# One layer-norm, Fourier-mixing and MLP block on one core: the MLP's products moved into one stretch of TensorE's program

## The reference

```python
x = box_conv_block(x)                       # layer 0
for l in range(4):                          # layer 1: four blocks
    residual = x                            # x is (4, 64, 128, 128)
    xn = layer_norm(x over channels)
    xf = rfft2(xn)
    o1 = relu(xf mixed by w1[l] over channels, complex)
    o2 = o1 mixed by w2[l] over channels, complex
    mask = (abs(o2.real) > 0.01) | (abs(o2.imag) > 0.01)
    x = residual + irfft2(o2 * mask)
    m = gelu(layer_norm(x) @ mlp_w1[l] + mlp_b1[l]) @ mlp_w2[l] + mlp_b2[l]   # 64 -> 256 -> 64
    x = x + m
x = box_conv_block(x); x = box_conv_block(x)   # layers 2 and 3
```

## Time and profile before

| | |
|---|---|
| device time, median of 3 runs (lowest to highest) | 3583.87 us (3582.81 to 3584.54) |
| the profiled execution, first to last instruction | 3583.9 us |
| TensorE busy | 3266.5 us (91%) |
| VectorE busy | 2413.5 us (67%) |
| ScalarE busy | 2339.5 us (65%) |
| GpSimd busy | 1656.8 us (46%) |
| mean granted TensorE clock | 0.964 of full speed |

### The profile page before, as it was taken

How to read it: one execution, slowest core, us unless ns; L and a number is a source line. 1 busy time by engine, 2 the same in 40 slices (tenths; PEclk the granted TensorE clock), 3 DMA queues, 4 the chain that set the end, 5 groups by cost and what they waited for, 6 DMA issues and landing times. The chain is left out here.

```text
span 3583.9 us, 53035 instructions
## 1 busy us (share of the span) xinstructions
PE 3266.5 (91%) x18285; PEld 1967.2 (55%) x18285; DVE 2413.5 (67%) x4148; ACT 2339.5 (65%) x3749; POOL 1656.8 (46%) x1389
## 2 busy tenths in 40 slices
PE   6946699999999999998999999999999999979689
PEld 2735464646474646464646464646464646334257
DVE  4956676767676667666767677677767674536677
ACT  3955576767676767677767676766666666646468
POOL 4445545454646454545454545555454543210242
PEclk7968899999999999999999999999999999989889
DMA  9850001010101010313120101111111111356898
GB/s 327 271 183 24 30 30 64 32 65 30 65 30 65 30 65 30 118 48 141 48 89 30 65 30 65 36 65 41 54 42 53 42 53 42 141 188 189 263 300 239
DMA packets 250281, 334.10 MB, mean 93 GB/s; under 512 B 22304, under 2 KB 195616, under 8 KB 242608
## 3 DMA queue, kind: packets, MB, share of 16 engines
q1 hardware_dynamic: 241664, 315.29, 26.0%
q0 software_dynamic: 7904, 15.57, 1.6%
q10 hardware_dynamic: 464, 0.02, 0.0%
HBM read 188.06 MB, written 142.74 MB: 92 GB/s over the span
## 5 line engine op out<-in xcount | busy, mean ns | idle before, releaser
L1546 ACT ACTIVATE images<-a_wide,a_up_b 128x1024 f32<-128x1024 f32 x512 | 569.0, 1111 | 137.0 <-PE a_wide L1728 135.6
L1728 PE MATMUL a_wide<-images 64*128 64x512 f32 x2048 | 579.9, 641 | 37.0 <-ACT images L1546 36.3
L1308 POOL TENSOR_TENSOR images<-a_o,a_mag 128x256 f32<-128x256 f32 (+1 forms) x512 | 365.1, 738 | 389.3 <-DVE a_mag L1410 389.3
L1739 PE MATMUL a_result<-images 128*64 128x512 f32 x2048 | 495.9, 604 | 32.5 <-DVE images L1421 32.3
L1266 POOL TENSOR_TENSOR images<-images,a_stat 128x512 f32<-128x512 f32 x256 | 268.5, 1050 | 520.1 <-DVEq L1455 503.0
L1393 DVE TENSOR_TENSOR a_o<-a_bank,a_mix_b 128x512 f32<-128x512 f32 (+1 forms) x272 | 181.4, 667 | 257.3 <-PE a_bank L1685 253.5
L1703 PEld LDWEIGHTS a_bank<-a_dft_h,a_g 128*128 128x128 f32 x2080 | 272.4, 191 | 129.0 <-issue 129.0
L1685 PEld LDWEIGHTS a_bank<-a_mix,a_o 128*128 128x128 f32 x2080 | 253.6, 192 | 152.8 <-issue 131.3
L1685 PE MATMUL a_bank<-a_mix,a_o 128*128 128x128 f32 x2080 | 299.1, 286 | 8.2 <-DVE a_o L1393 4.2
L1739 PEld LDWEIGHTS a_result<-images 128*64 128x64 f32 x2048 | 128.0, 136 | 314.1 <-issue 291.1
L1440 DVE TENSOR_REDUCE a_stat<-a_sq 128x16 f32<-128x1024 f32 x240 | 290.6, 1211 | 9.3 <-ACT a_sq L1580 8.3
(11 more groups left out here) (204 smaller groups left out, 6235.2 us busy)
## 6 DMA issues: line engine op xcount, KB each, us to landing
rows<-images SPq DMA_DIRECT2D x112, 512.0 KB, 2.8
images<-rows SPq DMA_DIRECT2D x105, 512.0 KB, 4.3
box_xc<-in_x SPq DMA_DIRECT2D x16, 1024.0 KB, 16.2
box_x<-in_x SPq DMA_DIRECT2D x64, 256.0 KB, 4.3
turned<-box_o SPq DMA_DIRECT2D x64, 256.0 KB, 3.6
images<-turned SPq DMA_DIRECT2D x16, 1024.0 KB, 12.4
planes<-box_work SPq DMA_DIRECT2D x64, 256.0 KB, 3.6
box_xc<-planes SPq DMA_DIRECT2D x16, 1024.0 KB, 19.0
```

Source lines behind the costliest of these rows:

```text
L1308: ins = G.tensor_tensor(y[n % 2][:, :, to].rearrange("p c k -> p k c"), o2[:, j % 3, lo:4, r], mask[:, lo:4], ALU.mult)
L1546: A(hidden[:, i % 2, j], wide[:], ACT.Gelu, bias=up_b2[:, l, j:j + 1]).then_inc(s_hid, 1)
L1728: mm = M(wide[:, half * BANK:(half + 1) * BANK], up_fold[cs, l, j * P:(j + 1) * P], yc[cs, i % 2], start=True, stop=True)
L1739: mm = M(result[half * C:(half + 1) * C, :], down[:, l, j, :], hidden[:, i % 2, j, half * BANK:(half + 1) * BANK], start=j == 0, stop=j == ...
```

## The change

The diff, cut to its core (left out: the removed semaphore, the helper `mask_of` and its use on GpSimd, the removed helpers `magnitude` and `other` of ScalarE):

```diff
@@ -1403,9 +1407,12 @@
 
                 def masks(n, j):
                     before = N_CHUNK * n
-                    k, top = chunk(j), mag[:, j % 2, :, 0]
-                    dve.wait_ge(s_mag, before + j + 1)
-                    V.tensor_tensor(top[:, 0:k], top[:, 0:k], mag[:, j % 2, 0:k, 1], ALU.max).then_inc(s_top, 1)
+                    k, top = chunk(j), mask_of(j)
+                    dve.wait_ge(s_o2, before + j + 1)
+                    if before + j >= 3:
+                        dve.wait_ge(s_masked, before + j - 2)
+                    V.tensor_reduce(top[:, 0:k], o2[:, j % 3, 0:k].rearrange("p k r c -> p k c r"), AX.X, ALU.max,
+                                    apply_absolute_value=True).then_inc(s_top, 1)
                     dve.wait_ge(s_top, 2 * (before + j) + 1)
                     V.tensor_scalar(top[:, 0:k], top[:, 0:k], THR, None, ALU.is_gt).then_inc(s_top, 1)
 
...
@@ -1420,25 +1427,27 @@
                     dve.wait_ge(s_back, i + 1)
                     V.tensor_tensor(x[:, row:row + HB], rows(result), x[:, row:row + HB], ALU.add).then_inc(s_res, 1)
 
-                def sum_up(r, kind, u):
+                def sum_up(r, kind, u, part):
                     if kind == 1:
                         n, k = divmod(r + 1, SETS)
-                        dve.wait_ge((s_x, s_x_up)[u], INVERSES * n + 2 * k + 2)
                         row = strip_row(k, u)
                         strip = x[:, row:row + SH]
                     else:
                         n, k = divmod(r + 7, SETS)
                         n -= 2
-                        if fresh(n):
+                        strip = strip_of(n, k, u)
+                    to = stat[:, part, r % SETS, kind - 1, u * SH:(u + 1) * SH]
+                    if part == 0:
+                        if kind == 1:
+                            dve.wait_ge((s_x, s_x_up)[u], INVERSES * n + 2 * k + 2)
+                        elif fresh(n):
                             dve.wait_ge(s_stage, 2 * (SETS * fresh_count(n) + k) + u + 1)
                         else:
                             dve.wait_ge(s_res, BLOCKS * n + 4 * k + 2 * u + 2)
-                        strip = strip_of(n, k, u)
-                    i = squares_before(r, kind, u)
-                    V.tensor_reduce(stat[:, 0, r % SETS, kind - 1, u * SH:(u + 1) * SH], strip, AX.X, ALU.add)
-                    dve.wait_ge(s_sq, i + 1)
-                    V.tensor_reduce(stat[:, 1, r % SETS, kind - 1, u * SH:(u + 1) * SH], squares_of(r, kind, u), AX.X, ALU.add
-                                    ).then_inc(s_sq_read, 1)
+                        V.tensor_reduce(to, strip, AX.X, ALU.add)
+                    else:
+                        dve.wait_ge(s_sq, squares_before(r, kind, u) + 1)
+                        V.tensor_reduce(to, squares_of(r, kind, u), AX.X, ALU.add).then_inc(s_sq_read, 1)
 
                 def root(r, js):
                     lo, hi = 0 if has_second(r + 1) else 1, 2 if has_first(r + 7) else 1
...
@@ -1460,18 +1469,24 @@
                         scale_weights()
                     if (n, q) == (-2, 10):
                         fold_weights()
-                    parts(n, q, 0, inverse, forward, spectrum, backward)
                     if 0 <= Q - 2 < BLOCKS * RUNS:
                         residual(Q - 2)
+                    parts(n, q, 0, inverse, forward, spectrum, backward)
                     if q == 14 and FIRST_ROOT <= r < END_ROOT:
                         root(r, range(ROOT_STEPS))
+                    late = 2 if q == 5 or q % 4 == 3 and fresh(n) else 1
                     for s in range(1, 4):
                         parts(n, q, s, inverse, forward, spectrum, backward)
-                        if s == (3 if q == 5 or q % 4 == 3 and fresh(n) else 1):
-                            for strip in (strips_at(n, 12)[1:] if q == 13 else []) + strips_at(n, q)[:1]:
-                                sum_up(*strip)
+                        strips = (strips_at(n, 12)[1:] if q == 13 else []) + strips_at(n, q)[:1]
+                        if s == late:
+                            for strip in strips[:-1]:
+                                sum_up(*strip, 0)
+                                sum_up(*strip, 1)
+                        if s - late in (0, 1):
+                            for strip in strips[-1:]:
+                                sum_up(*strip, s - late)
                         if FIRST_ROOT <= r < END_ROOT:
-                            if q == 1 and s == 1:
+                            if q == 1 and s == 2:
                                 root(r, range(ROOT_STEPS))
                             if (q, s) in ((5, 3), (9, 2)):
                                 root(r, range(ROOT_STEPS // 2))
...
@@ -1593,21 +1594,15 @@
 
                 for n, q in periods():
                     Q = BLOCKS * n + q
-                    mlp = 0 <= Q < BLOCKS * RUNS
-                    if mlp:
+                    if 0 <= Q < BLOCKS * RUNS:
                         gelu(Q, 0)
-                    parts(n, q, 0, inverse, forward, spectrum, backward)
                     if 0 <= Q + 1 < BLOCKS * RUNS:
                         operand(Q + 1)
-                    parts(n, q, 0, other, other, magnitude, other)
+                    parts(n, q, 0, inverse, forward, spectrum, backward)
                     if q != 12 and not (q % 4 == 3 and fresh(n)):
                         for strip in strips_at(n, q):
                             square(*strip)
                     parts(n, q, 1, inverse, forward, spectrum, backward)
-                    if q == BACKWARD_SLOT // 4 - 1:
-                        parts(n, q, 1, other, other, magnitude, other)
-                    if mlp:
-                        gelu(Q, 1)
                     if q == 12:
                         for strip in strips_at(n, q)[:1]:
                             square(*strip)
...
@@ -1616,17 +1611,15 @@
                             fill_stage(n, q // 4, 0)
                         for strip in strips_at(n, q):
                             square(*strip)
-                    if q != BACKWARD_SLOT // 4 - 1:
-                        parts(n, q, 1, other, other, magnitude, other)
                     parts(n, q, 2, inverse, forward, spectrum, backward)
-                    if 0 <= Q - 1 < BLOCKS * RUNS:
-                        mlp_delta(Q - 1)
-                    parts(n, q, 2, other, other, magnitude, other)
                     parts(n, q, 3, inverse, forward, spectrum, backward)
-                    parts(n, q, 3, other, other, magnitude, other)
+                    if 0 <= Q < BLOCKS * RUNS:
+                        gelu(Q, 1)
                     if q == 12:
                         for strip in strips_at(n, q)[1:]:
                             square(*strip)
+                    if 0 <= Q - 1 < BLOCKS * RUNS:
+                        mlp_delta(Q - 1)
                     if q % 4 == 0:
                         m, k = (n, q // 4 - 1) if q else (n - 1, SETS - 1)
                         if -2 <= m and m + 2 < RUNS and fresh(m):
...
@@ -1756,24 +1749,18 @@
 
                 for n, q in periods():
                     Q = BLOCKS * n + q
-                    mlp = 0 <= Q < BLOCKS * RUNS
-                    if mlp:
-                        mlp_up(Q, 0)
-                    if q != BACKWARD_SLOT // 4:
-                        parts(n, q, 0, inverse, forward, spectrum, backward)
                     if 0 <= Q - 2 < BLOCKS * RUNS:
                         turn_back(Q - 2)
                     if 0 <= Q + 1 < BLOCKS * RUNS:
                         turn(Q + 1)
-                    if q == BACKWARD_SLOT // 4:
-                        parts(n, q, 0, inverse, forward, spectrum, backward)
-                    parts(n, q, 1, inverse, forward, spectrum, backward)
-                    if mlp:
+                    for s in range(4):
+                        parts(n, q, s, inverse, forward, spectrum, backward)
+                    if 0 <= Q < BLOCKS * RUNS:
                         mlp_up(Q, 1)
-                    parts(n, q, 2, inverse, forward, spectrum, backward)
                     if 0 <= Q - 1 < BLOCKS * RUNS:
                         mlp_down(Q - 1)
-                    parts(n, q, 3, inverse, forward, spectrum, backward)
+                    if 0 <= Q + 1 < BLOCKS * RUNS:
+                        mlp_up(Q + 1, 0)
         clear(nc, sems)
         nc.all_engine_barrier()
 
```

More of the change, by code:

```diff
@@ L1087, in afno_layers @@
         s_fh, s_xf, s_mix1, s_o1, s_mix2, s_o2 = (sem(n) for n in ("fh", "xf", "mix1", "o1", "mix2", "o2"))
-        s_mag, s_top, s_masked, s_sym, s_ends = (sem(n) for n in ("mag", "top", "masked", "sym", "ends"))
+        s_top, s_masked, s_sym, s_ends = (sem(n) for n in ("top", "masked", "sym", "ends"))
         s_ih, s_iy = sem("ih"), [sem("iy_dve"), sem("iy_act")]
@@ L1102, in squares_of, with mask_of @@
             return mag[:].rearrange("p t k r c -> p (t k r) c") if in_mag(r, kind, u) else sq[:]
+        def mask_of(j):
```

(15 more changed lines are left out.)

## The result

The changed kernel takes 3684.5 us (median of 4 runs, 3681.6 to 3691.0) against 3584.2 beside it on the same chip: a ratio of 1.028 (1.027 to 1.030), slower, 15 us above the predicted 3669 and inside its range. The profiled execution has a span of 3679.8 us, 95.9 more than before.

What follows compares the result with a forecast made beforehand. TensorE, busy 171.0 of 176.3 us per run, sets the pace. Terms sum to +5.85 us per run, +88 over 15 runs, +3 fresh input, -4 ahead of the first image, -2 last run: +85, 3669 us; range 3614 to 3713.

Steps and rivals of the forecast that it cites:

- Periods 0 to 4, +1.1: Net per run: +2.8 us at period 4's inverse-to-forward turn, against an earlier turn; bounds 0 to +1.8.
- T: Moment in period 4 when TensorE's turn waits for GpSimd's normalise (1154.63 before); predicted to come 1.6 to 1.7 us earlier.
- Period 5, +2.2: Forward to spectrum: a 2.4 us hole before the first spectrum product, less two borders; bounds 1.9 to 2.5.
- Period 6, +0.8, and period 10, +0.8: Period 6: first, short slots wait for evacuations; period 10: the transposes' 0.93 comes on top, less one border.
- Periods 7 to 9, 0: Four spectrum slots in a row at pitch 2.80: 11.14 us against 11.17 before, so no gain.
- Period 11, -0.15: Backward was to lose borders between products of different tile shape alone, saving 0.15 us per run.
- Periods 12 and 13, +1.1: Inverse 2 waits, next first up 0.15 late, period 13's turn back 0.7 late: together +1.1 us (0.3 to 1.4).
- Around the runs, -4 and -2: Shorter queues ahead of the first image, -4 us; the last run has periods 0 and 1's gain alone, -2 us.
- The clock: Rival: holes of periods 4 and 5 lower the clock, some 8 us per run at low level; 3729 us; chance 0.06.
- Masks and sums, 0: Dropping ScalarE's Abs, VectorE's reduction (0.61 to 0.67 us) for its maximum, halving the sum: cost 0, sums charged elsewhere.
- the borders win: Rival: engines keep ahead, only TensorE's border savings are left, 4.4 us per run; 3518 us; chance 0.11.
- they cancel: Rival: chains of periods 4 and 12 are looser, so losses and gains balance; about 3584 us; chance 0.03.

Runs made afterwards that it cites:

- the two spread kernels: Changed kernel with the order of before in periods 4, 5, 6, 10, 12, 13 and fresh runs: 3560.5 us; likewise in periods 7 to 9: 3558.2 us.

## Why the prediction was right, and where it was off

The forecast was slower by 85 us, through holes where up and down used to stand; it was 96 by the span. By its steps:

- **Periods 0 to 4, +1.1:** measured +1.4. The two ends were both nearly right: T comes 1.35 earlier (27.94 us after the run's first up, before 29.29; I took 1.6 to 1.7), and from T to the next first up it is 13.67 against 10.91 (+2.8, as predicted). Forward group 2 starts at T + 8.36 (8.3 predicted).
- **Period 5, +2.2:** +2.0, with a hole of 2.36 for the weight load (2.4 predicted). The sum ahead of the memset is 0.4 of it, by the run that moved it.
- **Period 6, +0.8, and period 10, +0.8:** +0.7 and +0.8.
- **Periods 7 to 9, 0:** 0; the pitch is 2.80. Halving ReLU, which takes the open load away, brings it to 2.65 to 2.70. The border price and the price of the load are thus both real, and they cancel.
- **Period 11, -0.15:** -0.5. It stays in the two kernels that have the new order in 11 and not in 10, 12 and 13 (19.3 and 19.4), and goes with the new masks alone (19.7), so it belongs to this period's order. It is borders alone, as I said, but I took too few: before, the backward products took 7.31 + 3.77 + 3.77 us from start to start, with an up and a down product between them, and after 14.38 in one piece (1279.04 to 1293.42). Four borders went, at 0.12 each.
- **Periods 12 and 13, +1.1:** +0.6 and +0.4. The two new waits:

```profile
1302.41 1.12 PE L1649 MATMUL a_bank<-a_g,a_idft_e 128*128 128x512 f32 x2 [0.35 <-DVE images L1371]
...
1308.89 0.65 PE L1747 MATMUL a_result<-ident,images 128*128 128x128 f32 x4 [0.30 <-ACT images L1560]
```

- **Around the runs, -4 and -2:** -4.1 ahead of the first image; in the last run -1.5, and -2.3 more behind the runs. The -4.1 is not the new order's: with the order of before there and the new masks the first up product comes at 411.2 to 413.6, with the new order at 411.0 to 412.9, against 415.5 in the one profile of the kernel before. What is left is for the masks and the spread of single executions, which these profiles don't part. The -2.3 is within that spread too (419.3 to 423.0 us behind the last run in the kernels with the new masks).

Together +5.5 per run, where I had 5.85. Fifteen such runs make 82.5, and with -4.1, -1.5 and -2.3 that is 75 of the 96 us. The other 21 are two terms that I had mis-sized.

**The clock.** I gave it a rival with 0.06, at 8 us of the low level per run, all or nothing. It came in part: one stretch of 3.4 us in 9 of 15 runs, seven of them usual runs. A granted clock under 1.00 in the runs was one of my own signs of being wrong, and it showed; it cost 11 us in the usual runs and not the 60 that I had given it. The thirteen usual runs are 9.6 us above 13 x 5.5, and those falls at 1.6 make 11 (run 0 stands 1.4 below the 5.5). The step that failed is that the holes of periods 4 and 5 are "shorter than that idleness in all" and so mostly harmless: a hole of 2.2 (1.8 in one run) in dense work was followed by a fall in 9 of 15 runs. What decides in which run it falls is open: run 4 and run 1 have the same hole, and with a hole shorter by 0.4, or with period 4 restored, the falls come in other runs and in another number.

**The fresh runs.** I charged +3 for both, for the copy and the square "in ScalarE's queue between slots". They take 11.7 above the usual 5.5 each (13.1 + 9.6 - 11). The failed step is that I looked at what the copy delays in the slots, and not at the GELU that the change puts behind it: TensorE waited 3.11 us in period 3 of run 6, where the clock fell too, and 3.11 and 3.13 at the end of period 15 of runs 6 and 7. Of the 11.7, 3.2 are the two falls in period 5. With the order of before there, both runs take what they took before or less.

**Masks and sums, 0.** The masks alone gave 5.7 us (0.9976 to 0.9995 of before), none of it in the usual runs, where 0 was right. The new masks' cost was right (659 ns on average, 0.61 to 0.67 predicted). I looked at the mean of the old one only, 640 ns, and not at its maximum. The halved sum was to keep o2 from queueing behind a whole one; it does, and it is worth 17 us: by the profiles, 0.8 per usual run in periods 7 to 9, and 0.6 in periods 4 and 5 together (undivided sums make period 4 longer by 1.6 and period 5 shorter by 1.0, as the fall of the clock moves from one to the other).

Against the rivals: "the borders win" would have had 3518, and "they cancel" 3584. The saving of borders is there, but only where no operand depends on ScalarE or VectorE between the products that were brought together. Kept to such places, it gives the two spread kernels 0.7% less time than before, and with ReLU halved 1.05%; about 0.15% of this came with the new masks alone.

## What to carry to other kernels

Products that stand between two dependent steps are cover, and bundling them to save mode changes sells that cover: price both from the timeline, period by period, and bundle only where the neighbours that become adjacent don't wait for each other's evacuation. When an instruction moves in a hand-written order, look at what it is now queued behind in the rarest case too, here the runs that store fresh input. Where two slots do stand side by side, signal the evacuation of a stationary operand in halves, and don't put a whole reduction ahead of an addition that TensorE waits for.

## What the runs showed of the hardware

- A single hole of TensorE of 1.8 to 2.2 us in a run at clock 1.00 can be followed by 3.4 us at half clock (0.50, the 1.2 GHz level), which costs 1.6 us. After the same hole of 2.20 us it fell in run 1 and not in run 4. Behind one of 2.06 us (period 4 with the new order and undivided sums) it fell in 13 of 15 runs of one kernel and in 9 of 15 of the other, and behind one of 1.83 us (period 5, sum behind the memset) in 6 of 15. Behind the 1.51 in period 4 of the changed kernel it fell in none of the usual runs.
- A reduction over 128x512 that reads each number once took 683 ns by its median and never more than 699, where a maximum of two 128x256 operands took 416 by its median and up to 2704. All long executions of the maximum overlap a GpSimd instruction. The kernel with the reduction, and without the Abs, is 5.7 us faster; which of the two edits gives that, and whether the hold-ups ever cost TensorE anything, no run shows. The comparison of 128x256, the same in both kernels, has one SBUF input and a median of 294 ns in both, and still had executions of 2762 before and 2394 after.
- ReLU of 128x512 in two instructions costs ScalarE 2.3 us per run (110.3 to 112.6) and TensorE gains 0.26 per period of four slots side by side (pitch 2.65 to 2.70 for 2.80), and nothing where MLP products stand between them.
